# Softmax denominators of the first key half: summed on VectorE before one matmul, instead of a matmul for every key tile

## The reference

```python
paths = sigmoid(x @ Wp + bp)                      # 8 heads, 5 path values each
agree = pq * pk + (1 - pq) * (1 - pk)             # query by key, for each of the 5
sim = cumprod(agree, axis=-1).sum(axis=-1) / 5    # causal mask: -inf above the diagonal
attn = softmax(sim, axis=-1)
x = layernorm(x + (attn @ V) @ Wo)                # V = x @ Wv, 8 heads of 32
h = silu(x @ w_gate.T / 127) * (x @ w_up.T / 127) # 768 hidden
x = layernorm(x + h @ w_down.T / 127)
```

## Time and profile before

| | |
|---|---|
| median of 3 runs | 829.33 us (827.42 to 830.38) |
| the profiled execution | 829.72 us, of which the span of the trace is 828.0 us |
| PE busy | 786.7 us, 95% of the span |
| DVE busy | 609.6 us, 74% |
| ACT busy | 453.8 us, 55% |
| POOL busy | 292.3 us, 35% |
| granted clock of PE | 0.989 of full speed over the span |

### The profile page before, as it was taken

How to read it: one execution, slowest core, us unless ns; L and a number is a source line. 1 busy time by engine, 2 the same in 40 slices (tenths; PEclk the granted TensorE clock), 3 DMA queues, 4 the chain that set the end, 5 groups by cost and what they waited for, 6 DMA issues and landing times.

```text
span 828.0 us, 14242 instructions
## 1 busy us (share of the span) xinstructions
PE 786.7 (95%) x5442; PEld 381.5 (46%) x5442; DVE 609.6 (74%) x1081; ACT 453.8 (55%) x705; POOL 292.3 (35%) x266
## 2 busy tenths in 40 slices
PE   6998999999999999999999999999999999799976
PEld 5452364443644445443644436444554435244343
DVE  2768876699667976789666996679767897558667
ACT  1655645667365655657456673656556574365422
POOL 0202342336224262244423362242622444134324
PEclk9999999999999999999999999999999999899999
DMA  7842555044720826125540437207260255301011
GB/s 226 198 126 77 127 138 144 1 95 95 194 77 1 179 74 157 50 51 129 142 139 1 108 83 193 77 1 179 77 153 1 52 127 139 91 1 27 26 26 53
DMA packets 81301, 79.39 MB, mean 96 GB/s; under 512 B 37712, under 2 KB 60496, under 8 KB 81232
## 3 DMA queue, kind: packets, MB, share of 16 engines
q1 hardware_dynamic: 81232, 78.46, 37.8%
HBM read 53.28 MB, written 16.78 MB: 85 GB/s over the span
## 4 chain that ended last, share of the span: by engine, by line
PE 56%; DVE 23%; issue 9%; ACT 5%; DMA 3%; SPq 1%; POOL 1%; DVEq 0%; POOLq 0%; ACTq 0%
PE slot L909 9%; PE ctx_ps L932 9%; PE misc L969 9%; PE misc L982 7%; PE misc L883 7%; PE misc L955 6%; DVE acc L629 6%; PE den_ps L938 5%; DVE work L730 4%; ACT probs L531 4%; DVE x L712 4%; DVE acc L626 3%; DVE work L738 1%; DMA xT_sb<-in_xT_dram 1%; SPq L381 1%
## 5 line engine op out<-in xcount | busy, mean ns | idle before, releaser
L531 ACT ACTIVATE probs<-slot 128x1024 f32<-128x1024 f32 (+3 forms) x384 | 290.2, 808 | 256.0 <-PE slot L909 236.5
L460 POOL TENSOR_SCALAR_AFFINE_SELECT probs<-probs 128x512 f32<-128x512 f32 x128 | 143.2, 1119 | 210.1 <-ACT probs L531 210.0
L474 POOL TENSOR_TENSOR work<-work 128x512 f16<-128x512 f32 x96 | 116.8, 1217 | 163.6 <-ACT work L551 163.6
L932 PE MATMUL ctx_ps<-probs,vz_sb 128*32 128x512 f32 (+3 forms) x1536 | 164.7, 501 | 2.6 <-DVE ctx_raw L639 2.6
L909 PE MATMUL slot<-query_stack,key_stack 128*128 128x512 f16 (+3 forms) x768 | 160.0, 329 | 4.5 <-ACT probs L531 3.9
L969 PE MATMUL misc<-x1T_hi,w_parts 128*128 128x512 f16 x358 | 138.5, 387 | 9.3 <-DVE phi_lo L606 3.8
L969 PE MATMUL misc<-x1T_lo,w_parts 128*128 128x512 f16 x358 | 138.2, 386 | 0.0
L909 PEld LDWEIGHTS slot<-query_stack,key_stack 128*128 128x128 f16 x768 | 56.3, 98 | 164.1 <-issue 119.3
L730 DVE SCALAR_TENSOR_TENSOR work<-work,misc 128x512 f32<-128x512 f32 x90 | 61.5, 683 | 66.3 <-ACT work L545 65.5
L629 DVE TENSOR_TENSOR acc<-acc,probs 128x1536 f32<-128x1536 f32 (+3 forms) x60 | 95.0, 1584 | 0.6 <-POOL probs L460 0.5
L938 PE MATMUL den_ps<-probs,ones 128*32 128x512 f32 (+3 forms) x800 | 82.5, 484 | 0.0
(11 more groups left out here) (75 smaller groups left out, 707.6 us busy)
## 6 DMA issues: line engine op xcount, KB each, us to landing
key_stack<-phi_dram SPq DMA_DIRECT2D x56, 256.0 KB, 5.8
query_stack<-phi_dram SPq DMA_DIRECT2D x56, 256.0 KB, 6.3
x_sb<-in_x_dram SPq DMA_DIRECT2D x8, 1024.0 KB, 5.4
out_dram<-x SPq DMA_DIRECT2D x15, 512.0 KB, 4.1
xT_sb<-in_xT_dram SPq DMA_DIRECT2D x7, 1024.0 KB, 5.0
phi_dram<-phi_hi SPq DMA_DIRECT2D x14, 256.0 KB, 2.0
phi_dram<-phi_lo SPq DMA_DIRECT2D x14, 256.0 KB, 2.3
key_stack<-phi_dram SPq DMA_DIRECT2D x16, 128.0 KB, 3.1
```

Source lines behind the costliest of these rows:

```text
L460: pool.affine_select(out=tile, in_=tile, compare_op=ALU.is_ge, fill=0.0, base=0, pattern=[[0, 4], [1, P]], channel_multiplier=-1).then_inc ...
L474: pool.tensor_tensor(hid_lo[:, n % M1, :], hid[:, n % HSLOTS, :], hid_hi[:, n % M1, :], ALU.subtract).then_inc(hid_lo_ready, 1)
L531: act.activation(probs[:, s % P_SLOTS, 2 * p:2 * p + 2, off:CH], slot[p][:, :, off:CH], ACT.Exp).then_inc(slot_drained[p], 1)
L932: mm = pe.matmul(ctx_ps[32 * k:32 * k + 32, off:CH], vz_sb[:, b % 2, j, 32 * h:32 * h + 32], probs[:, s % P_SLOTS, k, off:CH], start=first ...
```

## The change

Chunks 0 and 1 of every batch but the first get the same treatment: all four of their tiles are added up on DVE, and four matmuls at the end of the chunk bring `acc` into `den_ps`, where they now start the accumulation instead of continuing it. Since the second tile is narrower than the first, the first sum is a copy of the first 128 columns of each head and an addition of the other 384. The sums of these chunks don't stand at the start of a slot but at places written into `BETWEEN`. The normalisation of the batch before (`norm(1, -1, 0)`) moves from slot 1 to slot 2, its `apply` and the store from slot 2 to between the two halves of the projection in slot 3, and the two feature computations of the next batch move from slots 6 and 8 to slots 10 and 11.

```diff
-    ADD_FROM = {2: 3, 3: 1}
+    ADD_FROM = {0: 0, 1: 0, 2: 3, 3: 1}
...
     def added(b, i):
-        return i in ADDED and i <= SUM_END[b, STEPS[i][0]]
-    NA = len(ADD_FROM)
+        q, c, g, j = STEPS[i]
+        return i in ADDED and not (b == 0 and c == 0) and not (b == B - 1 and q == NQ - 1 and i in DIAG)
...
-        1: down(-1, 0, 1) + norm(1, -1, 0),
-        2: vz(1, 0, 1) + [("apply", 1, -1, 0), ("store", -1, 0)],
-        3: project(-1, 1) + norm(0, -1, 1),
-        4: vz(1, 2, 3, 4) + [("load_x", 0), ("apply", 0, -1, 1), ("bias", 1, 0)] + turn_x1(-1, 1) + [("squash", 1, 0)],
+        1: down(-1, 0, 1),
+        2: vz(1, 0, 1) + norm(1, -1, 0) + [("sum", 0, 1)],
+        3: (project(-1, 1)[:2] + [("apply", 1, -1, 0), ("store", -1, 0)] + project(-1, 1)[2:] + norm(0, -1, 1)
+            + [("sum", 0, 2)]),
+        4: (vz(1, 2, 3, 4) + [("load_x", 0), ("apply", 0, -1, 1), ("bias", 1, 0), ("sum", 0, 3)] + turn_x1(-1, 1)
+            + [("squash", 1, 0)]),
         5: vz(1, 5),
-        6: vz(1, 6, 7) + gate_pair(-1, 6) + [("load_xT", 2), ("features", 1, 0), ("bias", 1, 1), ("squash", 1, 1)],
-        7: gate_pair(-1, 7) + halves(-1, 6),
-        8: gate_pair(-1, 8) + halves(-1, 7) + [("features", 1, 1)],
+        6: vz(1, 6, 7) + gate_pair(-1, 6) + [("load_xT", 2), ("bias", 1, 1), ("squash", 1, 1), ("sum", 0, 5)],
+        7: gate_pair(-1, 7) + halves(-1, 6) + [("sum", 0, 6)],
+        8: gate_pair(-1, 8) + halves(-1, 7) + [("sum", 0, 7)],
         9: gate_pair(-1, 9) + halves(-1, 8),
-        10: gate_pair(-1, 10) + halves(-1, 9),
-        11: project(0, 0) + halves(-1, 10) + norm(0, 0, 0),
+        10: gate_pair(-1, 10) + halves(-1, 9) + [("features", 1, 0)],
+        11: project(0, 0) + halves(-1, 10) + norm(0, 0, 0) + [("features", 1, 1)],
...
-                    dve.tensor_tensor(acc[:, :, :], probs[:, (s - 1) % P_SLOTS, :, :], own, ALU.add).then_inc(summed, 1)
+                    if SUMMED[b, q]:
+                        dve.wait_ge(acc_used, SUMMED[b, q])
+                    first = probs[:, (s - 1) % P_SLOTS, :, :]
+                    if off:
+                        dve.tensor_copy(acc[:, :, 0:off], first[:, :, 0:off])
+                    dve.tensor_tensor(acc[:, :, off:CH], first[:, :, off:CH], own, ALU.add).then_inc(summed, 1)
...
+                    alone = ADD_FROM[q] == 0
+                    if alone and NQ * b + q >= 1:
+                        pe.wait_ge(den_out, NQ * b + q)
                     for k in range(4):
-                        mm = pe.matmul(den_ps[32 * k:32 * k + 32, :], ones[:, :], acc[:, k, :], start=False, stop=final)
+                        mm = pe.matmul(den_ps[32 * k:32 * k + 32, :], ones[:, :], acc[:, k, :], start=alone, stop=final)
```

More of the change, by code:

```diff
@@ L46, in seq_postln_kernel @@
     DIAG = [i for i, (q, c, g, j) in enumerate(STEPS) if j >= TC * c]
-    ADD_FROM = {2: 3, 3: 1}
+    ADD_FROM = {0: 0, 1: 0, 2: 3, 3: 1}
     ADDED = [i for i, (q, c, g, j) in enumerate(STEPS) if q in ADD_FROM and j >= ADD_FROM[q]]
     ADDS = [i for i in ADDED if STEPS[i][3] > ADD_FROM[STEPS[i][0]]]
-    SUM_END = {(b, q): max(i for i in ADDED if STEPS[i][0] == q and not (b == B - 1 and q == NQ - 1 and i in DIAG))
-               for b in range(B) for q in ADD_FROM}
     def added(b, i):
-        return i in ADDED and i <= SUM_END[b, STEPS[i][0]]
-    NA = len(ADD_FROM)
+        q, c, g, j = STEPS[i]
+        return i in ADDED and not (b == 0 and c == 0) and not (b == B - 1 and q == NQ - 1 and i in DIAG)
+    SUM_END = {(b, q): max(i for i in ADDED if STEPS[i][0] == q and added(b, i))
+               for b in range(B) for q in ADD_FROM if any(STEPS[i][0] == q and added(b, i) for i in ADDED)}
+    SUMS = {at: n for n, at in enumerate((b, i) for b in range(B) for i in ADDS if added(b, i))}
+    SUMMED = {at: n for n, at in enumerate(SUM_END)}
     LAST = {q: max(i for i, s in enumerate(STEPS) if s[0] == q) for q in range(NQ)}
@@ L144, in between @@
             n[at] += b
+            if what == "sum" and tuple(n) not in SUMS:
+                continue
             if 0 <= n[at] < B and (what not in ("load_x", "load_xT", "stack") or n[at] > 0):
@@ L166, in seq_postln_kernel @@
         10: vz(1, 4, 5) + [("features", 1, 0)],
+        11: project(0, 0) + norm(0, 0, 0),
         12: vz(1, 6, 7) + [("apply", 0, 0, 0), ("load_xT", 2), ("bias", 1, 1), ("squash", 1, 1)],
@@ L180, in attention @@
                 plan += [("mask", b, i)]
-        if s >= 1 and (s - 1) % NS in ADDS and added(*divmod(s - 1, NS)):
-            plan += [("sum", *divmod(s - 1, NS))]
-        plan += between(b, i)
+        sums = [("sum", *divmod(s - 1, NS))] if s >= 1 and divmod(s - 1, NS) in SUMS else []
+        plan += between(b, i) if STEPS[(s - 1) % NS][1] == 0 else sums + between(b, i)
         if LAG <= s < B * NS - 1:
@@ L527, in exps @@
                         i2 += i2 not in ADDS
-                        act.wait_ge(summed, len(ADDS) * b2 + ADDS.index(i2) + 1)
+                        act.wait_ge(summed, SUMS[b2, i2] + 1)
                 for p in range(2):
@@ L615, in add_up @@
                 own = probs[:, s % P_SLOTS, :, off:CH]
-                count = len(ADDS) * b + ADDS.index(i)
+                count = SUMS[b, i]
                 if i in DIAG:
@@ L622, in add_up @@
                 if j == ADD_FROM[q] + 1:
-                    used = NA * b + list(ADD_FROM).index(q)
-                    if used:
-                        dve.wait_ge(acc_used, used)
-                    dve.tensor_tensor(acc[:, :, :], probs[:, (s - 1) % P_SLOTS, :, :], own, ALU.add).then_inc(summed, 1)
+                    if SUMMED[b, q]:
[4 more added lines that the diff above has]
+                    dve.tensor_tensor(acc[:, :, off:CH], first[:, :, off:CH], own, ALU.add).then_inc(summed, 1)
                 else:
@@ L634, in normalise @@
                 dve.wait_ge(pv_done, NS * b + LAST[q] + 1)
-                if q in ADD_FROM:
-                    dve.wait_ge(acc_used, NA * b + list(ADD_FROM).index(q) + 1)
+                if (b, q) in SUMMED:
+                    dve.wait_ge(acc_used, SUMMED[b, q] + 1)
                 if Q >= 1:
@@ L941, in weigh @@
                 if added(b, i) and i == SUM_END[b, q]:
-                    pe.wait_ge(summed, len(ADDS) * b + ADDS.index(i) + 1)
+                    pe.wait_ge(summed, SUMS[b, i] + 1)
+                    alone = ADD_FROM[q] == 0
+                    if alone and NQ * b + q >= 1:
+                        pe.wait_ge(den_out, NQ * b + q)
                     for k in range(4):
-                        mm = pe.matmul(den_ps[32 * k:32 * k + 32, :], ones[:, :], acc[:, k, :], start=False, stop=final)
+                        mm = pe.matmul(den_ps[32 * k:32 * k + 32, :], ones[:, :], acc[:, k, :], start=alone, stop=final)
                     mm.then_inc(acc_used, 1)
```

## The result

The changed kernel takes 834.98 us as a median of 6 runs (834.24 to 837.71), the kernel before 829.65 us (6 runs, 827.42 to 830.58). The ratio is 1.0074, with a 95% interval of 1.0054 to 1.0095: slower by 0.7%. The quotient of the two medians alone is 1.0064, inside that interval. The prediction was 837.2 us, slower, with 834 to 841 as the forecast's own range. The profiled execution took 836.84 us, its span is 835.1. One of the 17 runs of the kernel before that stand beside the first four experiments was slow, 1002.38 us at a granted clock of 0.754: it counts in no ratio, and without it their median of 829.77 us would be 829.61.

A forecast was written before the change was run, and what follows sets the result against it. PE was taken as the bound, without margin at slot 6's gate matmuls. Per batch 1.83 us lost less 0.7 gained, 1.13, times 7 is 7.9; on 829.72 that gives 837.6, median 837.2 us, forecast range 834 to 841.

The forecast's parts named there:

- The bound: Slot 6's gate matmuls: PE arrives about when transposed x1 does, so whatever makes x1 later shows on PE in full.
- DVE's replay: DVE's queue from chunk 3's denominators to x1: x1_hi starts at 325.88 instead of 324.05, gate matmuls 1.83 us later.
- the first `rsqrt`: On POOL, for the other normalisation: shut out until the first sum's end at 316.85, ends at 317.72.
- the first `apply`: Other normalisation's apply on DVE, behind the first residual: waits for its rsqrt, starts 317.72, takes 1.68 us.
- more of it: Rival: rsqrt between copy and addition delays the sum 0.9 us, or slots 7, 8 lengthen 0.3; 843 us, chance 0.13.
- The copy: First part of chunk 0's first sum on DVE, 128 columns for 4 heads (512 values): 0.40 us.
- the last `apply`: On DVE, behind the second rsqrt and ahead of x1_hi: takes 1.77 us, ends at 325.83.
- The second rsqrt: On POOL, beside chunk 0's second sum: shut out by the sum, ends 0.87 us after it, at 324.02.
- Slots 6 to 9: Late exponentials and tanh make PE wait 0.6 us at slot 8's gate matmuls; chunk 1 gains 0.7 us, not 1.30.
- The features: Moved to slots 10 and 11, 1.99 us on DVE: fall into DVE's waits and cost nothing.
- The sum: Whole program: 1.13 us longer per batch, times 7 is 7.9 us, giving a median of 837.2 us.

The follow-up runs named there:

- first four experiments: Four kernels: only chunk 1 summed; only chunk 0 summed; second sum ahead of second residual; chunk 1's first sum ahead of hidden values: 825.94, 841.23, 836.40, 830.32 us.
- e1_chunk1: The change with only chunk 1 summed on DVE and slots 1 to 4 as in the kernel before; 825.94 us, ratio 0.9954.
- e2_chunk0: The change with only chunk 0 summed on DVE, all else as in the change; 841.23 us, ratio 1.0152.
- e3_sum2_ahead: The change with chunk 0's second sum put ahead of the second residual and its statistics; 836.40 us, ratio 1.0082.
- e8_sum2_behind: The change with chunk 0's second sum put behind the apply that waits for rsqrt, next to the third sum; 834.96 us, ratio 1.0063.
- e10_features_only: The kernel before with only the two feature computations moved to slots 10 and 11; 829.43 us, ratio 0.9996.
- e5_moves_only: The change with no tile of chunks 0 and 1 summed, only the moved normalisation and features left; 826.70 us, ratio 0.9966.
- e7_norm_late: The change with chunk 1's first sum early, chunk 0's second sum ahead of the second residual, norm(1, -1, 0) in slots 8 and 9; 824.27 us.

## Why the prediction was right

**The bound.** That PE has no margin at slot 6's gate matmuls was right. `e1_chunk1` and `e2_chunk0` show it from both sides: what makes x1 late costs in full, and chunk 0's 1.30 us off PE brings nothing while x1 is late.

**DVE's replay.** From the end of chunk 3's denominators (310.04 + 0.90 = 310.94 in the chain of waits after) `x1_hi` starts at 15.67 us. The prediction said 16.11, before it was 14.28. The price was 1.39 us and not 1.83. (From start to start in the timelines, as in the table, it is 1.44 at `x1_hi` and 1.45 at the gate matmuls.) Most of the 0.44 us is one term: the first `rsqrt` was not shut out. It started under the copy and ended in 1.12 us, so the first `apply` never waited (0.26 us). I had it shut out until the addition's end; it ran under the short copy in front of the addition and on into the addition. That is the first half of what the rival "more of it" had foreseen; its second half, that the sum is held up, didn't come: the addition took 1.75 us, as it does in slot 6 without POOL beside it. The copy was 0.34 us from start to start, not 0.40, and the last `apply` 0.1 shorter.

**The second rsqrt.** Predicted to end 0.87 us after the sum; it ended 0.86 us after it. So close a hit is in part luck: the 0.87 had been read from a mask that counted from the recorded end of its sum, and the replay set it behind the start of the next instruction, 0.08 us before that. From the sum's start it is 2.00 us predicted and 2.09 measured. The contention that the Trainium skill states ("GPSIMD Engine Reference", section "1. Specifications") agrees with the trace's 1.92 us. `e3_sum2_ahead` and `e8_sum2_behind` show that the sum's place makes it, for `rsqrt` takes 1.01 us in both, and `e8_sum2_behind` what it is worth: 0.92 us at `x1_hi`.

**Slots 6 to 9.** The mechanism was right: `gated` ended at 338.90 + 0.69 - 332.24 = 7.35 us behind the gate start (predicted 7.3), and PE had to wait for it. The gain was 0.41 us and not 0.7, since slot 8's gate matmuls started 0.88 us later than PE could have, not 0.6. They started 339.64 - 332.24 = 7.40 us behind the gate start. For PE alone the prediction had 8.20 - 0.86 - 0.65 = 6.69 us, with 8.20 from the chain of waits. There a start that PE did not wait for is the modelled end of the work before it; the timeline of before has the same start 0.17 us earlier:

```profile
336.83 1.04 PE L909 MATMUL slot<-query_stack,key_stack 128*128 128x512 f16 x4
337.70 0.38 PE L969 MATMUL misc<-x1T_hi,w_parts 128*128 128x512 f16 x1
```

So PE alone needed 337.70 - 329.67 - 0.86 - 0.65 = 6.52 us, it lost 7.40 - 6.52 = 0.88, and 1.30 - 0.88 is 0.42. The prediction also had no wait of the scores of slot 8 for the same late exponentials. PE lost 0.27 us of the 0.88 there (337.11 to 338.16, where such a group ahead of scores takes 0.78, as from 318.20 to 318.98) and 0.61 at the gate matmuls (338.16 to 339.64, where scores take 0.87, as from 342.05 to 342.92). This second wait adds nothing to the sum, since the gate matmuls wait for `gated` in either case. The rows' own idle times, 0.20 and 0.45, give 0.65, since they count from the end of a matmul that otherwise overlaps the next.

**The features** cost nothing, as predicted: DVE still idled 0.40 us ahead of slot 12's `gated`, and `e10_features_only` is within 0.1% of before.

**The sum.** 1.13 us a batch were predicted, the traces show 1.04. Counted as in the table, the delay of x1 was put 0.38 us too high (1.83, measured 1.45) and chunk 1's gain 0.29 too high (0.70, measured 0.41). These are two separate errors, and it is luck that they nearly cancel. Times 7 the table gives 7.3 us, and the medians differ by 5.3. Of the missing 2 us the two traces show 1.85 at the program's end: from the issue of `x1_lo` in the last batch's slot 6 to the end of the span the change takes 113.43 us and the kernel before 115.69, 2.26 less, of which 0.41 is chunk 1's gain and counted already. The sum had the end at nothing. One trace of each tells this only roughly: the stretch up to the first issue of `x1_lo`, too, is between 74.9 and 77.5 us long in the twelve traces. `e5_moves_only` is 2.7 us faster by the same stretch, but how much of it is the moved normalisation in the change itself is not shown: `e2_chunk0` moves it too, has 113.74 us there, and its median is still 1.3 us above what its batches give. Nor is it shown what lower granted clocks cost in the batches of the change (0.980 to 0.986 in its six runs). So the direction, the place and the size in a batch were right; that the measured time came within 2.2 us of the 837.2 owes something to errors that cancel.

## What to carry to other kernels

Work taken off the busiest engine pays only behind the last wait that is already tight: look for the place where its input lands just in time, and do nothing that delays that input. An order written by hand deserves one question for each entry ahead of such a place: does anyone wait for this? Moving one normalisation of 3.3 us that only fed a store, one sum into idle time and one sum ahead of the second residual turned a loss of 0.7% into a gain of 2.1%. Moved work needs idle time where it lands: with the normalisation's two pieces in slots 8 and 9 instead of 6 and 8, 1.98 us of a batch were lost again. And when a time is taken as the difference of two starts, both should come from the same view: the chain of waits and the timeline differ by up to 0.2 us for the same instruction.

## What the runs showed of the hardware

- `rsqrt` on POOL (4 values a partition) took 1.92 us when a DVE addition with two SBUF operands had begun 0.17 us before it, and 1.12 us when it began under a copy of 512 values with the addition 0.16 us behind. Alone it took 1.01. In the second case POOL finished in the middle of the addition, and the addition was not longer (1.75 us). The two cases differ in which of the two had begun first; that this alone decides it, and how much of its work POOL had done before the addition began, no run shows.
- An SBUF to SBUF copy of 512 float32 values took 0.43 us, 0.34 from start to start.
- At the last batch's wait for the transposes PE's granted clock went to the half level for some us in eleven of the twelve traces; in `e7_norm_late` it stayed at 1.00, although PE's idle time ahead of the gate matmuls was 2.79 us there and 2.74 before.
- An idle time in a row of PE understates a wait by up to 0.16 us: 0.45 in the row, 0.61 from start to start.
